# A fused decoder layer on one core: divisions of cross attention in odd steps behind two masks, roundings moved in self attention, square roots behind the second maxima

## The chip, the cores and the metric

One Trainium2 chip, one of its cores. The metric is the time of one execution in device microseconds (us); three executions of a kernel give a median. The engines are TensorE (PE), VectorE (DVE), ScalarE (ACT), GpSimd (POOL) and SyncE (SP), which here only issues transfers. Inputs lie in device memory; PE writes into PSUM, the others mostly into SBUF.

## The reference

A decoder layer on x of 4 x 512 tokens x 512, float32:

```python
x = layernorm(x + attn(x, wq, wk, wv, wo))            # 16 heads of 32, rotary, causal, 8 k/v heads
x = layernorm(x + xattn(x, ctx_512, Wq, Wkv_expand, Wout))   # 16 heads, context of 1601 x 128,
                                                             # only its first 512 keys pass the causal mask
w1, w2, w3 = (nf4_roundtrip(w) for w in (weight1, weight2, weight3))   # 1408 x 512 each
x = layernorm(x + (silu(x @ w1.T) * (x @ w2.T)) @ w3.T)
```

The selection of key blocks in self attention keeps all of them, so both attentions are softmax(q k / sqrt(32) + causal mask) v. `nf4_roundtrip` quantises the three weights: 64 values share a scale, scales are quantised to int8, and each value goes to the nearest of 16 levels, which takes 15 comparisons.

## The kernel before

The work is cut in 8 blocks b of 512 tokens: 0 to 3 are the self attention of the four sequences, 4 to 7 their cross attention (`crossed(b)` is b >= 4, `late(b)` is b >= 3). A block has 8 steps p, one for each pair of heads; a step is written (b, p) here. The feed-forward part, 4 tiles of tokens by 11 of hidden units, follows (7,7). Beside the attention of a step run pieces of other blocks' work: projections of the next block, the output projection and layer norm of the block before, and the quantisation of the weights. Every engine has its own program, written out by hand in a fixed order and tied to the others by semaphores, so an instruction that waits holds up all that stands behind it on its engine.

A step on PE, in order: the transposed scores of its units 0 and 1 (`scores`, L1014, a unit is one head's half of the queries, with the row's maximum subtracted by an extra row of the stack), maxima 0 of the step two further on (`maxima`, L978: scores whose row maximum DVE takes), the last two units of the step before weighted with the values (`weigh`, L1041), the maxima turned into rows (L1002), maxima 1, scores 2 and 3, then the projection of the next block in two halves (`make`, L962 to L964) with maxima 2 and 3 ahead of, between or behind the halves, weigh 0 and 1, and last the rounding (`rounding`, L1159: 16 small matmuls in bf16 that add up the comparisons' results). The banks of `att_scores_T` are two; scores, turned maxima, projections and roundings go through them as a ring (`ring_order`), and each must be emptied by ACT or DVE first.

DVE takes the maxima (L1653 in self attention, L1648 with the mask in cross attention), the reciprocals of the sums (`sums_of`, `over_sums`, L1660 to L1671), its share of the comparisons (`exceeds`, L1808), the layer norm: the square root by some 14 steps on 128 x 4 numbers (`begin_spread`, `end_spread`, L2054 to L2079) and the scaling (`scale_rows`, L1704). ACT has the exponentials (`exponential`, L1461, four in a step), the copies of sums (L1469) and of projections (L1386, L1399), and the other comparisons (`exceed`, L1439). The comparisons need rows that SP loads (`load_rows4`, L512) ahead of each rounding. POOL has the causal masks of cross attention (`keep_causal`, L842, one for each exponential), the division by the sums (`weighed`, L806, L808, L810), the rotary products, the division of the weights by their scales, and, in block 7, casts for the feed-forward part (L858).

SP issues the transfers of the stacks, six for each pair (`load_stacks`, L491 to L499, upper parts first, then lower), the rows, the results of the rounding (L525) and others, in the order of its program. `round_steps` (L104) gives the roundings to steps: 20 in self attention, the others in cross attention.

## Time and profile before

| | us |
|---|---|
| median of three executions | 1119.15 |
| lowest, highest | 1118.89, 1129.97 |
| the profiled execution: its own time | 1125.64 |
| its span in the trace | 1123.9 |
| PE busy | 1038.3 |
| DVE, ACT, POOL busy | 755.5, 482.4, 439.8 |

The profile is of one execution. An engine's idle time ahead of an instruction is given with what released it. TensorE's clock is granted by the chip at one of two levels, 1.2 or 2.4 GHz; the profile shows it as a share of the full one, 0.50 or 1.00, and over the whole execution it is 0.976. Matmuls are pipelined, so the spans of two that follow each other overlap.

### The profile page before, as it was taken

To read this page: it belongs to the slowest core of one execution; us is meant where nothing else is said; L and a number is where in the kernel's file an instruction comes from. 1 tells how busy PE (TensorE), PEld (TensorE's weight loads), DVE (VectorE), ACT (ScalarE), POOL (GpSimd) and SP (SyncE) were. 2 spreads that over 40 slices of the span, in tenths; PEclk is the share of its full clock that TensorE was granted. 3 is DMA by queue.
4 is the path that set the end of the run, shared out by engine and by line. 5 is a ranking of instruction groups with operands and counts; after the bars stand their busy time and mean duration, and the time that the engine had idled before them with its cause. 6 is when DMAs were issued, how large, how long until landed. Compare 5 with 4: busy or idle time off the path is not lost.

```text
span 1123.9 us, 17522 instructions
## 1 busy us (share of the span) xinstructions
PE 1038.3 (92%) x6280; PEld 670.4 (60%) x6280; DVE 755.5 (67%) x1560; ACT 482.4 (43%) x587; POOL 439.8 (39%) x462
## 2 busy tenths in 40 slices
PE   9899999999999898998989998998989999999995
PEld 7545455555455454565546556555636888888884
DVE  7778658666866688559676876877673546464535
ACT  3343445554464464546654664676442212112110
POOL 3448675975786564123352432334257000000000
PEclk9899999999999999999989999999989999999998
DMA  6731586386636674646755485757445202011021
GB/s 232 216 91 30 140 220 180 90 242 179 191 84 169 189 203 102 160 92 147 208 140 125 116 202 127 166 147 183 111 135 163 83 1 105 8 38 38 1 75 38
DMA packets 92618, 145.16 MB, mean 129 GB/s; under 512 B 22507, under 2 KB 39795, under 8 KB 92275
## 3 DMA queue, kind: packets, MB, share of 16 engines
q1 hardware_dynamic: 83218, 116.49, 39.8%
q0 software_dynamic: 8000, 26.75, 8.3%
q8 instruction: 51, 0.84, 0.3%
q10 hardware_dynamic: 1312, 0.79, 0.2%
q14 instruction: 37, 0.30, 0.1%
HBM read 78.09 MB, written 23.73 MB: 91 GB/s over the span
## 4 chain that ended last, share of the span: by engine, by line
PE 67%; DVE 19%; issue 5%; DMA 3%; POOL 3%; ACT 2%; SPq 1%; ACTq 0%; DVEq 0%; POOLq 0%
PE att_pv L1041 11%; PE att_scores L978 7%; PE att_scores L1294 7%; PE att_pv L1294 7%; PE att_scores_T L1324 7%; PE att_scores_T L962 6%; PE att_scores_T L1014 5%; PE att_scores_T L964 5%; PE att_scores_T L963 5%; DVE att_mx L1653 4%; PE att_scores_T L1159 2%; DVE att_scores L1648 2%; DVE att_nf_zone L1808 2%; DMA att_nf_home<-nf_reciprocals 2%; DVE att_stats L1684 1%
## 5 line engine op out<-in xcount | busy, mean ns | idle before, releaser
L1461 ACT ACTIVATE att_probs<-att_scores_T 128x1024 f32<-128x1024 f32 (+2 forms) x256 | 218.3, 885 | 161.7 <-PE att_scores_T L1014 159.1
L1041 PE MATMUL att_pv<-att_probs,att_v 128*32 128x512 f32 (+3 forms) x1024 | 216.6, 539 | 7.9 <-POOL att_probs L842 7.1
L1041 PE MATMUL att_pv<-att_probs,att_ones 128*32 128x512 f32 (+3 forms) x1024 | 216.6, 539 | 0.0
L1653 DVE TENSOR_REDUCE att_mx<-att_scores 128x2 f32<-128x1024 f32 x124 | 151.5, 1222 | 86.1 <-PE att_scores L978 85.3
L978 PE MATMUL att_scores<-att_k_stack,att_q_stack 96*128 96x256 f32 (+1 forms) x504 | 168.8, 407 | 32.2 <-DVE att_mx L1653 23.1
L1648 DVE CUSTOM_DVE_ANT_0 att_scores<-att_scores,att_cmask 128x128 f32<-128x128 f32 (+3 forms) x256 | 120.9, 511 | 40.6 <-PE att_scores L978 39.4
L1014 PE MATMUL att_scores_T<-att_q_stack,att_k_stack 97*128 97x512 f32 (+2 forms) x512 | 140.3, 386 | 7.7 <-ACT att_raw L1399 2.3
L978 PEld LDWEIGHTS att_scores<-att_k_stack,att_q_stack 96*128 96x128 f32 x504 | 88.3, 195 | 80.5 <-DVE att_mx L1653 32.8
L842 POOL TENSOR_SCALAR_AFFINE_SELECT att_probs<-att_probs 128x256 f32<-128x256 f32 x128 | 59.0, 461 | 164.8 <-ACT att_probs L1461 159.5
L1014 PEld LDWEIGHTS att_scores_T<-att_q_stack,att_k_stack 97*128 97x128 f32 x512 | 87.7, 195 | 49.4 <-issue 18.9
L1547 ACT ACTIVATE att_probs<-att_scores 128x512 f32<-128x512 f32 x44 | 26.3, 598 | 208.0 <-PE att_scores L1294 208.0
L1041 PEld LDWEIGHTS att_pv<-att_probs,att_v 128*32 128x32 f32 x1024 | 48.4, 112 | 107.3 <-issue 80.0
L1971 DVE TENSOR_TENSOR att_probs<-att_probs,att_pv 128x512 f32<-128x512 f32 x44 | 30.2, 687 | 110.0 <-PE att_pv L1294 110.0
L806 POOL TENSOR_TENSOR att_pv_raw<-att_pv_raw,att_sums_turned 128x512 f32<-128x512 f32 x32 | 42.1, 1315 | 90.7 <-DVE att_sums_turned L1671 72.1
L1439 ACT ACTIVATE att_nf_zone<-att_probs,att_nf_limits 128x1408 bf16<-128x1408 bf16 x37 | 54.2, 1464 | 39.2 <-DMA att_probs<-nf_x 39.2
L962 PE MATMUL att_scores_T<-att_x_hi,att_w_hi 128*128 128x512 f32 x144 | 58.7, 408 | 0.2 <-ACT att_probs L1461 0.2
L962 PE MATMUL att_scores_T<-att_w_hi,att_o_hi 128*128 128x512 f32 x128 | 52.1, 407 | 7.0 <-ACT att_probs L1461 3.8
L964 PE MATMUL att_scores_T<-att_x_hi,att_w_lo 128*128 128x512 f32 x144 | 56.8, 394 | 0.0
L963 PE MATMUL att_scores_T<-att_x_lo,att_w_hi 128*128 128x512 f32 x144 | 56.7, 394 | 0.0
L964 PE MATMUL att_scores_T<-att_w_hi,att_o_lo 128*128 128x512 f32 x128 | 50.7, 396 | 0.0
L963 PE MATMUL att_scores_T<-att_w_lo,att_o_hi 128*128 128x512 f32 x128 | 50.6, 395 | 0.0
L1399 ACT ACTIVATE att_raw<-att_scores_T 128x1024 f32<-128x1024 f32 x35 | 35.8, 1024 | 32.7 <-PE att_scores_T L964 32.7
(262 smaller groups left out, 2102.3 us busy)
## 6 DMA issues: line engine op xcount, KB each, us to landing
att_q_stack<-att_q_hi SPq DMA_DIRECT2D x128, 128.0 KB, 3.2
att_probs<-nf_x SPq DMA_DIRECT2D x28, 352.0 KB, 3.5
att_nf_home<-nf_reciprocals POOLq DMA_DIRECT2D x48, 176.0 KB, 4.8
att_q_stack<-att_q_lo SPq DMA_DIRECT2D x64, 128.0 KB, 3.6
att_k_stack<-att_k_hi SPq DMA_DIRECT2D x64, 128.0 KB, 3.5
att_nf_home<-nf_x SPq DMA_DIRECT2D x20, 352.0 KB, 3.6
w_nf<-att_nf_zone SPq DMA_DIRECT2D x192, 22.0 KB, 2.5
att_k_stack<-att_k_hi SPq DMA_DIRECT2D x64, 64.0 KB, 4.1
```

Source lines behind the costliest of these rows:

```text
L842: pool.affine_select(out=v, in_=v, compare_op=ALU.is_ge, fill=0.0, base=0, pattern=[[0, 2], [1, P]], channel_multiplier=-1).then_inc(kept, 1)
L962: T.matmul(out, a_hi, b_hi, start=start, stop=False)
L963: T.matmul(out, a_hi, b_lo, start=False, stop=False)
L964: return T.matmul(out, a_lo, b_hi, start=False, stop=stop)
L978: last = T.matmul(sco[:, r, 0:width], qst[0:96, s, r, P * t:P * t + P], kst[0:96, r if crossed(b) else 0, s, 0:width], start=True, stop=True)
L1014: last = T.matmul(bank[:, at:at + S - q0], kst[0:97, r if crossed(b) else 0, s, P * t:P * t + P], qst[0:97, s, r, q0:S], start=True, stop= ...
L1041: last = T.matmul(pv[HD * j:HD * j + HD, sums, q0:S], lhs, pr[:, at:at + S - q0], start=(t == 0), stop=(t == TT - 1))
L1294: last = T.matmul(bank, ffn_weight(w, f, kt), x[:, kt, :], start=kt == 0 and i == 0, stop=kt == KT - 1 and i == 1)
L1324: last = T.matmul(fpy[:, t, :], h[:, g % 2, P * t:P * t + P], ffn_rows(f), start=f == 0 and i == 0, stop=f == FT - 1 and i == 1)
L1461: A.activation(probs_of(b, r)[:, 1024 * h:1024 * h + w], bank[:, 0:w], ACT.Exp, scale=SCALE).then_inc(st_free, 1)
L1648: V.tensor_tensor_reduce(out=sco[:, r, 0:width], in0=sco[:, r, 0:width], in1=cmask[:, S - width:S], scale=1.0, scalar=NEG, op0=ALU.add, op ...
L1653: V.tensor_reduce(mx[:, p % 2, :].rearrange("p (r t) -> p r t", r=2)[:, :, t], sco[:, :, :], AX.X, ALU.max).then_inc(sc_free, 1)
```

## The change

1. `round_steps`: in blocks 1 to 3 pair 0 is left out, in place of pair 5. The roundings of (2,0) and (3,0) go; (1,5) and (2,5) get one, and those between move up by one.
2. SP, (4,5), (5,5), (6,5): the four transfers of the upper parts of the next block's first stack are issued ahead of the rows, the two of the lower parts stay behind.
3. POOL, cross attention: the division goes from the end of an even step (2, 4, 6) to the odd step behind it, between masks 0, 1 and masks 2, 3.
4. PE, start: 15 matmuls of the identity with itself, whose result nothing reads, in groups of five ahead of maxima 1, 2 and 3 of (0,1).
5. PE and DVE, block 3: maxima 2 stand ahead of the projection and maxima 3 between its halves, as in cross attention; on DVE they are taken before sums and comparisons.
6. ACT, cross attention, pairs 3 and 6: the first comparison goes behind exponential 3.
7. DVE: in blocks 1 and 2 the square root stands whole behind maxima 0 and 1 of pair 2, and the scaling at the step's end; in block 3 at pair 3, behind maxima 1 and 2, with the scaling of (3,4) in halves behind maxima 2 and behind the comparisons.

```diff
@@ round_steps
-            if b < B and p == 5 or b == B - 1 and p > 4 or (b, p) in ((1, 0), (B, 0)):
+            if b < B and p == 0 or b == B - 1 and p > 4 or (b, p) == (B, 0):
@@ SP
-            def load_stacks(b, p):
+            def load_stacks(b, p, parts=(0, 1)):
...
-                for lo in range(2):
+                for lo in parts:
...
+                    if fresh and crossed(b):
+                        load_stacks(*nxt, (0,))
...
                     if fresh:
-                        load_stacks(*nxt)
+                        load_stacks(*nxt, (1,) if crossed(b) else (0, 1))
@@ POOL
                         keep_causal(b, p, 0)
                         keep_causal(b, p, 1)
+                        if p > 1 and p % 2:
+                            weighed(pairs(b, p) // 2 - 1)
...
                         keep_causal(b, p, 2)
                         keep_causal(b, p, 3)
-                    if p % 2 == 0 and pairs(b, p) > 2 or (b, p) == (0, 3):
+                    if p % 2 == 0 and pairs(b, p) > 2 and not (crossed(b) and p > 0) or (b, p) == (0, 3):
                         weighed(pairs(b, p) // 2 - 1)
@@ PE
             for t in range(1, TT):
+                for i in range(5):
+                    T.matmul(bank_for(("exp", 0, 0, 0))[:, 0:P], ident[:, :], ident[:, :], start=True, stop=True)
                 maxima(0, 1, t)
...
-                    elif crossed(b) and whats:
+                    elif late(b) and whats:
@@ ACT
-                    elif 0 in mine:
+                    behind = crossed(b) and p in (3, 6)
+                    if mid is None and 0 in mine and not behind:
                         exceed(end, 0)
                     exponential(b, p, 3)
+                    if mid is None and 0 in mine and behind:
+                        exceed(end, 0)
@@ DVE
                         moments(b - 1, 1)
-                        if not late(b):
-                            begin_spread(range(TT))
...
-                    if b > 0 and not late(b) and p == 2:
-                        end_spread(range(TT))
-                    if b == B - 1 and p == 3:
-                        begin_spread(range(TT))
-                    if (b, p) == (B - 1, 4) or (b, p) == (NB - 1, 5):
+                    if (b, p) == (NB - 1, 5):
                         scale_rows(range(0, 2), TT - 1)
                     if fore:
                         maxima(*fore, 1)
...
                     if b > 0 and not late(b) and p == 2:
-                        scale_rows(range(TT), TT - 1)
-                    quick = crossed(b) and bool(made(b + 1, p))
+                        spread(range(TT))
+                    quick = late(b) and bool(made(b + 1, p))
                     if quick:
                         maxima(*fore, 2)
-                    if crossed(b) and p == 3:
-                        begin_spread(range(TT))
                     if late(b) and p == 3:
-                        end_spread(range(TT))
+                        spread(range(TT))
...
-                    if quick and b > B and p == 5:
+                    if quick and (b > B and p == 5 or (b, p) == (B - 1, 4)):
                         scale_rows(range(0, 2), TT - 1)
...
                     exceeds(end, (1, 2, 3) if beside else (3,))
...
+                    if b > 0 and not late(b) and p == 2:
+                        scale_rows(range(TT), TT - 1)
```

How the rows stand, at three places. First DVE in step (1,2); (2,2) is alike. `att_newton` is the square root, `att_mx` the maxima. Before:

```order
L2075 SCALAR_TENSOR_TENSOR att_newton<-att_newton 128x4 [waits att_seq]
L2077 TENSOR_TENSOR att_newton<-att_newton 128x4 [waits att_seq]
L2079 SCALAR_TENSOR_TENSOR att_newton<-att_newton 128x4 [waits att_seq]
L1653 TENSOR_REDUCE att_mx<-att_scores 128x2 [waits att_sc_full]
L2075 SCALAR_TENSOR_TENSOR att_newton<-att_newton 128x4 [waits att_seq]
L2077 TENSOR_TENSOR att_newton<-att_newton 128x4 [waits att_seq]
L2079 SCALAR_TENSOR_TENSOR att_newton<-att_newton 128x4 [waits att_seq]
L2075 SCALAR_TENSOR_TENSOR att_newton<-att_newton 128x4 [waits att_seq]
L2077 TENSOR_TENSOR att_newton<-att_newton 128x4 [waits att_seq]
L2079 SCALAR_TENSOR_TENSOR att_newton<-att_newton 128x4 [waits att_seq]
L1653 TENSOR_REDUCE att_mx<-att_scores 128x2 [waits att_sc_full,att_seq]
L1704 TENSOR_SCALAR att_y<-att_y,att_mean_var,att_newton 128x512 x4
```

Now, with line numbers of the changed kernel:

```order
L1696 BN_STATS att_stats<-att_y 128x6
L1665 TENSOR_REDUCE att_mx<-att_scores 128x2 [waits att_sc_full] x2
L2058 MEMSET att_newton 128x4 [waits att_seq]
L2060 BN_AGGR att_mean_var<-att_stats 128x2 x4
L2067 TENSOR_SCALAR att_newton<-att_mean_var 128x4 [waits att_seq]
L2069 TENSOR_SCALAR att_newton_int<-att_newton 128x4 [waits att_seq]
L2071 TENSOR_SCALAR att_newton<-att_newton_int 128x4 [waits att_seq]
L2079 SCALAR_TENSOR_TENSOR att_newton<-att_newton 128x4 [waits att_seq]
L2081 TENSOR_TENSOR att_newton<-att_newton 128x4 [waits att_seq]
L2083 SCALAR_TENSOR_TENSOR att_newton<-att_newton 128x4 [waits att_seq]
L2079 SCALAR_TENSOR_TENSOR att_newton<-att_newton 128x4 [waits att_seq]
L2081 TENSOR_TENSOR att_newton<-att_newton 128x4 [waits att_seq]
```

The maxima that stood between the steps of the root and behind them stand ahead of it, and the scaling of `att_y` has gone from here to behind the last comparison of the step.

Second SP in step (4,5). `att_probs<-nf_x` are the rows, `w_nf<-att_nf_zone` the results of the rounding before. Before:

```order
L512 DMA att_probs<-nf_x 128x1x1408 [waits att_piece_out1,att_piece_out0,att_st_full]
L525 DMA w_nf<-att_nf_zone 32x352 [waits att_round_ok]
L525 DMA w_nf<-att_nf_zone 32x352 x3
L519 DMA att_probs<-nf_dequantised_rows 128x352 [waits att_dqr_out1]
L491 DMA att_q_stack<-att_q_hi 32x2x512 [waits att_st_free,att_st_full]
L491 DMA att_q_stack<-att_q_hi 32x2x512
L495 DMA att_k_stack<-att_k_hi 32x2x512 x2
L491 DMA att_q_stack<-att_q_lo 32x2x512 [waits att_cross_raw_cut]
L495 DMA att_k_stack<-att_k_lo 32x2x512
L669 DMA att_y<-w_cross 128x4x512 [waits att_y_out]
```

Now:

```order
L491 DMA att_q_stack<-att_q_hi 32x2x512 [waits att_st_free,att_st_full]
L491 DMA att_q_stack<-att_q_hi 32x2x512
L495 DMA att_k_stack<-att_k_hi 32x2x512 x2
L512 DMA att_probs<-nf_x 128x1x1408 [waits att_piece_out1,att_piece_out0,att_st_full]
L525 DMA w_nf<-att_nf_zone 32x352 [waits att_round_ok]
L525 DMA w_nf<-att_nf_zone 32x352 x3
L519 DMA att_probs<-nf_dequantised_rows 128x352 [waits att_dqr_out1]
L491 DMA att_q_stack<-att_q_lo 32x2x512 [waits att_cross_raw_cut,att_st_full]
L495 DMA att_k_stack<-att_k_lo 32x2x512
```

The first four transfers of the stack stand ahead of the rows; the last two stay.

Third POOL from (7,2) to (7,5), with the casts L858 (L860 now) between. AFFINE_SELECT is the masks, four to a step. Before:

```order
L842 AFFINE_SELECT att_probs<-att_probs 128x2x128 [waits att_probs_kept,att_st_free] x4
L806 TENSOR_TENSOR att_pv_raw<-att_pv_raw,att_sums_turned 128x512 [waits att_o_ok,att_o_over_sums]
L808 CAST att_o_hi<-att_pv_raw 128x512 [waits att_o_divided]
L810 TENSOR_TENSOR att_o_lo<-att_pv_raw,att_o_hi 128x512 [waits att_o_hi_ok]
L858 CAST att_w_hi<-att_rope_tab 128x1024 [waits att_ffn_w_ok,att_ffn_w_in1]
L842 AFFINE_SELECT att_probs<-att_probs 128x2x128 [waits att_probs_kept,att_st_free] x4
L858 CAST att_w_lo<-att_rope_tab 128x1024 [waits att_ffn_w_ok,att_ffn_w_in2]
L858 CAST att_w_lo<-att_c_in 128x1024 [waits att_ffn_w_ok,att_ffn_w_in0]
L842 AFFINE_SELECT att_probs<-att_probs 128x2x128 [waits att_probs_kept,att_st_free] x4
```

Now:

```order
L844 AFFINE_SELECT att_probs<-att_probs 128x2x128 [waits att_probs_kept,att_st_free] x4
L860 CAST att_w_hi<-att_rope_tab 128x1024 [waits att_ffn_w_ok,att_ffn_w_in1]
L844 AFFINE_SELECT att_probs<-att_probs 128x2x128 [waits att_probs_kept,att_st_free] x2
L808 TENSOR_TENSOR att_pv_raw<-att_pv_raw,att_sums_turned 128x512 [waits att_o_ok,att_o_over_sums]
L810 CAST att_o_hi<-att_pv_raw 128x512 [waits att_o_divided]
L812 TENSOR_TENSOR att_o_lo<-att_pv_raw,att_o_hi 128x512 [waits att_o_hi_ok]
L844 AFFINE_SELECT att_probs<-att_probs 128x2x128 [waits att_probs_kept,att_st_free] x2
L860 CAST att_w_lo<-att_rope_tab 128x1024 [waits att_ffn_w_ok,att_ffn_w_in2]
L860 CAST att_w_lo<-att_c_in 128x1024 [waits att_ffn_w_ok,att_ffn_w_in0]
L844 AFFINE_SELECT att_probs<-att_probs 128x2x128 [waits att_probs_kept,att_st_free] x6
```

Before, the division (the three rows on `att_pv_raw`, `att_o_hi`, `att_o_lo`) stands between the masks of two steps; now it stands between the first and the second two of the odd step.

## Rows read from the trace of the kernel before

**Rows 1.** The page's first part: busy us (share of the span) and instructions.

```profile
PE 1038.3 (92%) x6280; PEld 670.4 (60%) x6280; DVE 755.5 (67%) x1560; ACT 482.4 (43%) x587; POOL 439.8 (39%) x462
```

**Rows 2.** Waits of PE: us in total, times, longest us.

```profile
PE att_scores L978 <- DVE att_mx L1653: 23.1, 33, 1.9
PE att_scores_T L1159 <- DVE att_probs L1808: 9.3, 16, 1.0
PE att_pv L1041 <- POOL att_probs L842: 7.1, 6, 2.0
PE att_scores L978 <- DMA att_k_stack<-att_k_lo: 2.5, 2, 1.4
```

**Rows 3.** Windows: length, busy us of PE, PEld, DVE, ACT, POOL; granted clock; DMA.

```profile
38.20:48.40 10.20, 8.32 (x21) 5.00 (x25) 7.34 (x11) 4.91 (x7) 0.00 (x0) 0.50 0.92 324
290.80:294.20 3.40, 3.40 (x12) 1.49 (x10) 3.33 (x8) 2.82 (x3) 1.52 (x1) 0.50 0.59 153
816.50:819.90 3.40, 2.96 (x16) 0.59 (x16) 3.06 (x11) 0.00 (x0) 2.19 (x4) 0.50 0.99 175
```

**Rows 4.** Timeline, PE at the start: start us, us, engine, line, operation.

```profile
1.59 6.65 PE L1185 MATMUL att_scores<-att_ident 128*128 128x128 f32 x32 [1.59 <-POOL att_ident L726]
...
36.92 0.73 PE L978 MATMUL att_scores<-att_k_stack,att_q_stack 96*128 96x512 f32 x2 [1.32 <-DVE att_mx L1653]
```

**Rows 5.** Timeline, block 2, pair 2.

```profile
288.95 0.15 DVE L2075 SCALAR_TENSOR_TENSOR att_newton<-att_newton 128x4 f32<-128x4 f32 x1
289.09 0.73 PE L978 MATMUL att_scores<-att_k_stack,att_q_stack 96*128 96x512 f32 x2 [1.34 <-DVE att_mx L1653]
```

**Rows 6.** Timeline, PE in steps (2,0) and (3,1).

```profile
260.42 0.33 PE L1159 MATMUL att_scores_T<-att_nf_zone,att_nf_steps 128*32 128x352 bf16 x4 [1.42 <-DVE att_nf_home L1808]
...
388.65 0.51 PE L962 MATMUL att_scores_T<-att_w_hi,att_o_hi 128*128 128x512 f32 x1 [1.79 <-POOL att_o_lo L810]
```

**Rows 7.** Timeline, PE in steps (3,3) and (3,4).

```profile
427.26 0.73 PE L978 MATMUL att_scores<-att_k_stack,att_q_stack 96*128 96x512 f32 x2 [1.21 <-DVE att_mx L1653]
...
439.95 0.74 PE L978 MATMUL att_scores<-att_k_stack,att_q_stack 96*128 96x512 f32 x2 [1.67 <-DVE att_mx L1653]
```

**Rows 8.** Timeline, steps (4,5) and (4,6).

```profile
540.42 1.00 ACT L1399 ACTIVATE att_raw<-att_scores_T 128x1024 f32<-128x1024 f32 x1
541.52 0.57 SPq L512 DMA_DIRECT2D att_probs<-nf_x  x1
...
545.56 1.46 ACT L1439 ACTIVATE att_nf_zone<-att_probs,att_nf_limits 128x1408 bf16<-128x1408 bf16 x1
...
553.02 0.50 PE L978 MATMUL att_scores<-att_k_stack,att_q_stack 96*128 96x256 f32 x2 [1.13 <-DMA att_k_stack<-att_k_lo]
```

**Rows 9.** Timeline, block 7, pairs 3, 5 and 7.

```profile
816.94 1.07 PE L1041 MATMUL att_pv<-att_probs,att_v 128*32 128x512 f32 x2 [1.88 <-POOL att_probs L842]
...
820.26 1.02 PE L978 MATMUL att_scores<-att_k_stack,att_q_stack 96*128 96x512 f32 x2 [0.18 <-DVE att_mx L1648]
...
833.80 1.07 PE L1041 MATMUL att_pv<-att_probs,att_v 128*32 128x512 f32 x2 [0.76 <-POOL att_probs L842]
...
843.04 1.29 POOL L806 TENSOR_TENSOR att_pv_raw<-att_pv_raw,att_sums_turned 128x512 f32<-128x512 f32 x1 [0.65 <-DVE att_sums_turned L1671]
843.74 2.92 ACT L1461 ACTIVATE att_probs<-att_scores_T 128x896 f32<-128x896 f32 x4 [1.88 <-PE att_scores_T L1014]
...
846.31 2.02 POOL L842 TENSOR_SCALAR_AFFINE_SELECT att_probs<-att_probs 128x256 f32<-128x256 f32 x4
...
847.31 1.07 PE L1041 MATMUL att_pv<-att_probs,att_v 128*32 128x512 f32 x2 [1.29 <-POOL att_probs L842]
```

**Rows 10.** Timeline, DVE's comparisons beside POOL and alone.

```profile
570.55 2.29 DVE L1808 TENSOR_SCALAR att_nf_zone<-att_probs,att_nf_limits 128x1408 bf16<-128x1408 bf16 x2
570.55 1.27 POOL L810 TENSOR_TENSOR att_o_lo<-att_pv_raw,att_o_hi 128x512 fp32r<-128x512 f32 x1
...
584.23 1.08 DVE L1808 TENSOR_SCALAR att_nf_zone<-att_probs,att_nf_limits 128x1408 bf16<-128x1408 bf16 x2
```

4 lines of the change are left out of this document (1 added, 3 removed).

## The prediction

> **What bounds the kernel now.** I read the page's busy times first: TensorE (PE) is busy 1038.3 us of 1123.9, so what a change can win is idle time of PE, its half-speed time, or nothing [rows 1]. PE's waits come next. The largest is for the second maxima, L1653 on VectorE (DVE), 23.1 us in 33 pieces; then 9.3 us for the comparisons of the rounding (L1808), 7.1 us in six pieces for the causal masks on GpSimd (POOL, L842), and 2.5 us in two pieces for the stacks [rows 2]. Each is an upper bound of what its part of the change can win. Third come the windows: in short stretches PE's clock is granted at 0.50, the lower of its two levels, 1.2 in place of 2.4 GHz [rows 3]. Each stood behind a gap: 1.32 us twice before 38.2, 1.34 us before 290.8, 1.88 us at 816.5 [rows 4, 5, 9]. A short stretch is 3.4 us long with PE busy all of it, so it costs 3.4 / 2 = 1.7 us where PE bounds. Nine more such stretches lie at 58.7, 389.8, 441, 553.7, 574.1, 656.1, 833.6, 847.2 and behind the end. So each gap that goes is priced twice: itself, and 1.7 us if a stretch stood behind it. Not every such gap had one: 1.42, 1.79 and 1.21 us are read below, and only the second was followed by one.
>
> The profiled execution took 1125.64 us, 6.5 above the median of 1119.15. I sum against the profile and subtract 6.5 at the end. Steps are written (block, pair).
>
> **A. Fifteen filler matmuls at the start.** The warming matmuls are the same operation: 16 of them in 6.65 us, at 0.50, so 0.42 each, 0.21 at full clock [rows 4]. Three groups of 5 are 1.04 us each. The first group stands where PE did not wait, so it delays everything by about 1.0. The other two fall into the two gaps of 1.32 [rows 4]. What they buy is the clock: the stretch from 38.2 is 10.2 us long with 8.3 us of matmuls [rows 3], 4.2 us at full clock. PE then waits for DVE and ScalarE (ACT) more often. DVE's 7.3 us of work in it sets how short it can get, 10.2 - 7.3 = 2.9 saved; none if it stays low, though then the fillers, twice as long, cost 2.1 for the first group. Bounds -1.9 and +2.1; I take **-1.5**, since three groups fill most of both gaps.
>
> By the Trainium skill ("TensorE: Matmul & The Clock Gate", Why this matters for your kernels) the clock drops only for PE-idle gaps above about 3 us; by it the fillers buy nothing and this part costs their 1.0. The trace disagrees: the longest of PE's waits is 2.0 us [rows 2], and the clock fell behind gaps of 1.3 to 1.9 [rows 3 to 5, 9].
>
> **B. Rounding moved off pair 5 in blocks 1 and 2, on to pair 0 skipped.** Twenty roundings stay. (2,0) and (3,0) lose a rounding of 0.8 us of matmuls and the wait ahead of it, 1.42 at 260.4 [rows 6] and a like one in (3,0); (1,5) and (2,5) get one each, with its row load, its comparisons and its stores on SyncE (SP). Removed 2 x 2.2 = 4.4, added 2 x (0.8 + a wait between 0 and 1.5). But in (3,1) PE waits 1.79 us for POOL's L810 [rows 6], and POOL there waits for its own transfers, so what (3,0) gains is lost again. Bounds -2.8 and +1.5; I take **-0.5**.
>
> **C. Square root behind the second maxima, blocks 1 and 2.** At 288.95 DVE runs the small steps of the root ahead of the maxima; PE then waits 1.34, and the low stretch at 290.8 follows [rows 5, 3]. In the new order three maxima stand ahead of the root and the scaling behind the comparisons. Removed in (2,2): 1.3 + 1.7 = 3.0; in (1,2) some 0.6 without a stretch. The same DVE work now stands ahead of maxima 3 and the sums, and bounds the loss at 1.0 for two steps. Bounds -3.6 and +1.0; I take **-2.6**.
>
> **D. Block 3 in the order of cross attention.** The gaps of 1.21 in (3,3) and 1.67 in (3,4) go [rows 7], the second with a stretch at 441. In their place the rounding waits: DVE does maxima 2, sums, comparisons, maxima 3 and one more comparison before it, two maxima later than now, at 1.2 us each. (3,2) has no gap today and gets one of about 1.5; in (3,4) about 2.2 comes back. Bounds: -1.2 - 1.7 - 1.7 = -4.6 if nothing comes back, +3 if both waits come and the stretch stays. I take **+0.5**.
>
> **E. Upper parts of the next stack ahead of the rows, (b,5) of blocks 4 to 6.** Rows' load L512 goes out at 541.52, at once when the rounding before it is done; the stack's first source is free when ACT has copied it, 540.42 + 1.00 = 541.42, no earlier. So four issues of 0.62 us now stand ahead, and the rows leave 2.5 us later. ACT uses them at 545.56, only just landed (3.96 us from issue) [rows 8]. Behind that comparison on ACT stand the fourth exponential, a second comparison and the two copies of the projection; those free the bank in which PE forms the next scores. So PE gets it 2.2 us later. On the other side the last lower part leaves at the same time as now, since as many issues stand ahead of it, but behind fewer bytes, and the stack's gap, 1.13 at 553.02 and 1.4 in block 5 [rows 8, 2], is covered by the new wait. So +2.2 - 1.13 = +1.1, +0.8, and in block 6, which has no stack gap, +2.2: together +4.1; a stretch stays behind each of the first two. If rows land as early as now: -1.13 - 1.4 - 2 x 1.7 = -5.9. If a new stretch comes in block 6 too: +5.8. I take **+3.5**.
>
> **F. Division in odd cross steps, behind two masks.** A division is three POOL instructions, from 843.04 until the masks start at 846.31 [rows 9], 3.3 us. Now masks 0 and 1 wait for it, afterwards masks 2 and 3. Block 7: (7,5) loses its 0.76 gap and the stretch, -2.4, for the second pair of masks is wanted late there. In (7,3) the 1.88 gap goes [rows 9], but the root's small steps on DVE now run beside the division all the way, and today already PE waits 0.18 at 820.26 for the maxima behind them. So the gap moves there: -0.5. In (7,7) nothing is left of the step to hide masks 2 and 3: of the four exponentials of 0.73 from 843.74 two belong to masks 0 and 1, so these end at 845.9, the division at 849.2 and mask 2 at 849.7; PE, with four pairs of matmuls of 0.43 at full clock from 846.0, is ready at 847.7. A new wait of 2.0 stands for the 1.29 that goes, started 1.29 earlier: -0.5. (4,7): 1.98 of gap shrinks, -0.8. Blocks 5 and 6: 0.6 each goes, 0.8 comes: +0.3. Comparisons and root beside the division in (b,3) and (b,7): +1.2. The price is read at 570.55: two comparisons take 2.29 beside POOL's L810, 1.08 alone [rows 10]. Sum **-2.7**. If every mask wait goes with its stretches: -7.1 - 4 x 1.7 = -13.9. If none and each of seven overlaps costs 1.2: +8.4.
>
> The Trainium skill ("SBUF — State Buffer", Who interferes with whom) says that a DVE instruction in a two-port mode and a GpSimd one block each other whole. The pair of rows at 570.55 agrees; by its text small single-input steps would not be held, while the rows of the root beside the division are.
>
> **G. One comparison behind the fourth exponential in pairs 3 and 6**: 1.46 us of ACT, released exponential earlier, masks earlier; bounds -1.5 and +0.5, taken **-0.2**.
>
> Sum: -1.5 - 0.5 - 2.6 + 0.5 + 3.5 - 2.7 - 0.2 = -3.5. 1125.6 - 3.5 = 1122.1 in the profile's terms, 1115.6 as a median.
>
> **Rivals.**
> 1. *The rows decide* (slower). All three steps (b,5) lose the full 2.5 us, and the wait of PE passes 1.3 us, so a stretch of 1.7 stands behind each: 3 x 4.2 = 12.6 in place of 3.5. It decides from the moment the rows land after ACT's third exponential (545.6 now, so with any delay over 0.2 us). For: no slack in that row; against: DVE comparisons may run first, and PE has projection work to do. Sum +5.6: 1124.8. With D's and F's upper bounds as well it would pass 1130.
> 2. *All stretches at changed places vanish* (faster). A -1.9, C -3.6, E -5.9, F -9 (block 7's three gaps and stretches), the rest as above: about -20, 1099. For: each stretch stands behind a gap that the change addresses; against: (7,3) and (7,7), where the gap only moves.
> 3. *The clock does not hang on these gaps.* The stretches stay where they are, fillers cost 1.0, gaps alone count: A +1.0, C -1.2, E +3.5, F -1.3, others 0: +2.0, 1121.2. Against: every stretch stands behind a gap; for: gaps of 1.42 and 1.21 had none. The page on the clock gate named above stands nearest to this one.
> 4. *Nothing moves*: PE runs on as now, as each gap turns into the next wait: 1119.
>
> **How the numbers follow.** Forecast 0.45, the rows 0.2, all vanish 0.13, no link to gaps 0.12, nothing 0.1. A measurement tells about 1%, 11.2 us: below 1108 or above 1130. Faster gets the second rival and a tail of the forecast, 0.18; slower the tail of the first and of F's contention, 0.1. The range leaves out the far part of either: 1104 to 1127.
>
> **What would show it.** After: no low stretch near 290; the fillers' two gaps filled and the clock at 1.00 through 38 to 48 (A); PE's masks row (L842) down from 7.1 to under 4, and the one left in (7,7) behind masks 2 and 3 (F); ACT idle before its first comparison at (4,5), (5,5), (6,5) for some 2 us with the rows as releaser, and no wait of PE for the k stack (E); the rounding's wait row up from 9.3 (D). Wrong if the stretches come elsewhere in the same number, or if ACT shows no such wait.

## The result and the profile after

The changed kernel takes 1154.11 us (median of four runs, 1148.11 to 1157.44); the kernel before took 1120.52 beside it. The ratio is 1.0255, 95% interval 1.0214 to 1.0296: slower by 2.6%. I had forecast 1115.6 and no change.

Below, a gap is idle time of PE ahead of an instruction, and a stretch is a time in which its clock was granted at 0.50. PE's busy time and waits in the changed kernel (us in total, times, longest), which answer to [rows 1] and [rows 2]; L1820 is the old L1808, L1665 the old L1653, L844 the old L842:

```profile
PE 1055.0 (91%) x6310; PEld 682.6 (59%) x6310; DVE 755.0 (65%) x1560; ACT 482.0 (42%) x587; POOL 430.5 (37%) x462
```

```profile
PE att_scores_T L1164 <- DVE att_probs L1820: 16.4, 14, 2.8
PE att_scores_T L1164 <- DVE att_nf_home L1820: 16.0, 6, 4.3
PE att_scores L983 <- DVE att_mx L1665: 15.5, 28, 1.9
...
PE att_pv L1046 <- POOL att_probs L844: 3.0, 2, 2.4
```

The two targets shrank as meant: maxima from 23.1 to 15.5, masks from 7.1 to 3.0. But the rounding's waits for DVE's comparisons grew from 12.2 (9.3 and 2.9) to 32.4. All gaps of PE over 0.15 us add up to 87.1 us, 71.9 before. Busy PE grew by 17 us although its work grew by 3, the fillers; the other 14 are matmuls that ran slower. Outside the end the trace has 88.7 us at 0.50, 47.8 before. So of the 31.8 us by which the profiled execution is longer, some 15 are waits, 3 fillers and 14 low clock. That is about a third of a us for each us at 0.50, not the half at which I priced it: over the 17 traces of this case PE's busy time without the fillers rises by 0.35 to 0.38 us for each us at 0.50 (a fitted line, an estimate, since the ends of matmuls are modelled). The trace is of the slowest of the four executions (1157.44 us, mean granted clock 0.958; the others have 0.961 to 0.971), so it holds more low clock than the median one.

Laid step beside step, most of the loss comes in three places: (1,5) and (2,5) grew from 8.8 to 14.9 and 14.5 us, (1,3) and (2,3) by 1.5 and 4.2, and (3,2) to (3,6) by 10.7 together. The timeline of (1,5):

```profile
224.46 2.37 POOL L781 TENSOR_TENSOR att_k_lo<-att_turned,att_k_hi 128x1024 fp32r<-128x1024 f32 x1
225.53 4.29 DVE L1820 TENSOR_SCALAR att_nf_zone<-att_nf_home,att_nf_limits 128x1408 bf16<-128x1408 bf16 x2
...
226.96 2.47 POOL L791 TENSOR_TENSOR att_turned<-att_raw,att_rope_tab 128x1024 f32<-128x1024 f32 x1
...
230.87 1.52 DVE L1820 TENSOR_SCALAR att_nf_home<-att_nf_home,att_nf_limits 128x1408 bf16<-128x1408 bf16 x1
232.09 2.52 POOL L796 TENSOR_TENSOR att_turned<-att_turned,att_swapped 128x1024 f32<-128x1024 f32 x1
232.54 1.07 PE L1164 MATMUL att_scores_T<-att_nf_zone,att_nf_steps 128*32 128x352 bf16 x12 [4.29 <-DVE att_nf_home L1820]
```

Two comparisons that take 1.08 us alone [rows 10] take 4.29 (singly 1.69 and 2.68), and each ends 0.4 us after a product of POOL: the first waits out L781 (to 226.83), the second L791 (to 229.43). PE idles as long, 4.29 us, and its clock is low afterwards. The windows behind the waits of the rounding in (1,5), (2,5), (3,3) and (3,4), 4.29, 3.87, 3.17 and 2.50 us, to be read as [rows 3]:

```profile
232.10:238.90 6.80, 6.36 (x32) 3.25 (x36) 3.25 (x4) 1.94 (x2) 6.50 (x7) 0.50 1.02 289
354.90:361.70 6.80, 6.31 (x32) 3.26 (x36) 3.25 (x4) 1.94 (x2) 6.42 (x7) 0.50 0.64 182
450.50:457.30 6.80, 5.71 (x30) 2.71 (x34) 4.86 (x7) 1.94 (x2) 0.00 (x0) 0.50 0.38 106
467.60:474.40 6.80, 6.43 (x34) 2.91 (x38) 5.40 (x7) 1.94 (x2) 4.76 (x5) 0.50 0.24 55
```

In (2,3) the scaling of the layer norm, which takes 1.91 us in (1,3) and 3.24 here, stands ahead of the rounding's last instruction on DVE (L1834), which frees the bank for PE's scores:

```profile
307.74 3.24 DVE L1716 TENSOR_SCALAR att_y<-att_y,att_mean_var,att_newton 128x512 f32<-128x512 f32 x4
...
312.63 0.50 DVE L1834 SCALAR_TENSOR_TENSOR att_nf_zone<-att_scores_T,att_nf_home 128x352 bf16<-128x352 f32 x1
...
313.19 0.73 PE L1019 MATMUL att_scores_T<-att_q_stack,att_k_stack 97*128 97x512 f32 x2 [2.51 <-DVE att_nf_zone L1834]
```

And in (3,3) the whole root, maxima 2 and 3 and three comparisons precede the rounding, slowed beside POOL: L2067 takes 1.36 us beside POOL's L816, 0.17 in the median of its 13.

```profile
441.83 2.55 POOL L816 TENSOR_TENSOR att_w_lo<-att_rope_tab,att_w_hi 128x512 fp32r<-128x512 f32 x2
...
443.06 1.36 DVE L2067 TENSOR_SCALAR att_newton<-att_mean_var 128x4 f32<-128x4 f32 x1
...
447.41 1.53 POOL L764 TENSOR_TENSOR att_nf_home<-att_nf_home 128x704 bf16<-128x704 bf16 x1 [1.55 <-DMA att_nf_home<-nf_reciprocals]
447.48 2.34 DVE L1820 TENSOR_SCALAR att_nf_zone<-att_nf_home,att_nf_limits 128x1408 bf16<-128x1408 bf16 x2
...
449.74 1.21 DVE L1665 TENSOR_REDUCE att_mx<-att_scores 128x2 f32<-128x1024 f32 x1
450.88 0.57 DVE L1820 TENSOR_SCALAR att_nf_home<-att_nf_home,att_nf_limits 128x1408 bf16<-128x1408 bf16 x1
451.59 1.07 PE L1164 MATMUL att_scores_T<-att_nf_zone,att_nf_steps 128*32 128x352 bf16 x12 [3.17 <-DVE att_nf_home L1820]
```

### The profile page after: what moved, and what is told of

Same layout as the page of the kernel before. It is cut to its first block, busy times and chain, and to the rows that moved or that the text cites. A ratio compares the mean times of both kernels' runs of the same rounds, so it can differ in the third digit from the quotient of the medians.

```text
span 1155.7 us, 17583 instructions
## 1 busy us (share of the span) xinstructions
PE 1055.0 (91%) x6310; PEld 682.6 (59%) x6310; DVE 755.0 (65%) x1560; ACT 482.0 (42%) x587; POOL 430.5 (37%) x462
## 4 chain that ended last, share of the span: by engine, by line
PE 67%; DVE 16%; DMA 5%; issue 4%; POOL 3%; ACT 3%; ACTq 0%; SPq 0%; DVEq 0%; POOLq 0%
PE att_pv L1046 11%; PE att_scores L983 7%; PE att_scores L1302 7%; PE att_pv L1302 7%; PE att_scores_T L1332 7%; PE att_scores_T L1019 6%; PE att_scores_T L967 6%; PE att_scores_T L969 5%; PE att_scores_T L968 5%; DVE att_mx L1665 3%; DMA att_nf_home<-nf_reciprocals 3%; DVE att_nf_zone L1820 2%; PE att_scores_T L1164 2%; DVE att_scores L1660 2%; DMA att_probs<-nf_x 1%
## 5 line engine op out<-in xcount | busy, mean ns | idle before, releaser
L1046 PE MATMUL att_pv<-att_probs,att_v 128*32 128x512 f32 (+3 forms) x1024 | 220.5, 547 | 3.2 <-POOL att_probs L844 3.0
L1665 DVE TENSOR_REDUCE att_mx<-att_scores 128x2 f32<-128x1024 f32 x124 | 151.6, 1223 | 107.2 <-PE att_scores L983 106.5
L1046 PE MATMUL att_pv<-att_probs,att_ones 128*32 128x512 f32 (+3 forms) x1024 | 220.4, 547 | 0.0
L983 PE MATMUL att_scores<-att_k_stack,att_q_stack 96*128 96x256 f32 (+1 forms) x504 | 171.5, 416 | 24.8 <-DVE att_mx L1665 15.5
L1019 PE MATMUL att_scores_T<-att_q_stack,att_k_stack 97*128 97x512 f32 (+2 forms) x512 | 148.9, 405 | 11.6 <-DVE att_nf_zone L1834 5.1
L983 PEld LDWEIGHTS att_scores<-att_k_stack,att_q_stack 96*128 96x128 f32 x504 | 91.2, 202 | 72.2 <-DVE att_mx L1665 27.2
L844 POOL TENSOR_SCALAR_AFFINE_SELECT att_probs<-att_probs 128x256 f32<-128x256 f32 x128 | 56.6, 442 | 206.2 <-ACT att_probs L1469 203.5
L1019 PEld LDWEIGHTS att_scores_T<-att_q_stack,att_k_stack 97*128 97x128 f32 x512 | 92.8, 206 | 56.5 <-issue 18.1
L1164 PE MATMUL att_scores_T<-att_nf_zone,att_nf_steps 128*32 128x352 bf16 x576 | 32.2, 330 | 32.7 <-DVE att_probs L1820 16.4
L1164 PEld LDWEIGHTS att_scores_T<-att_nf_zone,att_nf_steps 128*32 128x32 bf16 x576 | 14.6, 98 | 63.3 <-issue 45.3
```

What stands on the lines that cost most here:

```text
L983: last = T.matmul(sco[:, r, 0:width], qst[0:96, s, r, P * t:P * t + P], kst[0:96, r if crossed(b) else 0, s, 0:width], start=True, stop=True)
L1019: last = T.matmul(bank[:, at:at + S - q0], kst[0:97, r if crossed(b) else 0, s, P * t:P * t + P], qst[0:97, s, r, q0:S], start=True, stop= ...
L1046: last = T.matmul(pv[HD * j:HD * j + HD, sums, q0:S], lhs, pr[:, at:at + S - q0], start=(t == 0), stop=(t == TT - 1))
L1164: last = T.matmul(bank[32 * j:32 * j + 32, 0:CW], nsteps[:, 32 * k:32 * k + 32], passes[k][:, CW * j:CW * j + CW], start=k == 0, stop=k == 3)
L1665: V.tensor_reduce(mx[:, p % 2, :].rearrange("p (r t) -> p r t", r=2)[:, :, t], sco[:, :, :], AX.X, ALU.max).then_inc(sc_free, 1)
```

## The experiments

Ratios are to the kernel before, run on the same chip beside the experiment, with their 95% intervals; the changed kernel's is 1.0255 (1.0214 to 1.0296). A difference of 0.1% is 1.1 us. The changed kernel was not run again beside the experiments, so they are compared with it by these ratios: the intervals of experiments 1, 2 and 9 lie clear of its own, that of experiment 8 touches it, and those of 3 to 7 and 10 overlap it, so there the traces tell more than the times.

**1. Roundings back** (s1). Edit of the changed kernel:

```diff
-            if b < B and p == 0 or b == B - 1 and p > 4 or (b, p) == (B, 0):
+            if b < B and p == 5 or b == B - 1 and p > 4 or (b, p) in ((1, 0), (B, 0)):
```

> The changed kernel with the roundings on their old steps (pair 5 of blocks 1 to 3 left out again, pair 0 of blocks 2 and 3 used). Theory 1: the moved roundings cost about 12.6 us of the 33 (steps (1,5) and (2,5) grew by 6.1 and 5.7, (1,6) and (2,6) by 1.1 each, (2,0) and (3,0) gave back 2.3 and 2.7, (2,1) took 2.8), because the comparisons of DVE stand beside POOL's rotary products there; so about 1142. Theory 2: the waits at (1,5) and (2,5) of 4.3 and 3.9 us are a delay that DVE carries from the moved root and scaling and would come out at another rounding; then the time stays above 1150.

1141.19 us, 1.0136 (1.0088 to 1.0184): 13 us come back, as theory 1 had it. (1,5) and (2,5) are 8.8 us again. The gap in (3,3), which the edit does not touch, is 4.60 in this trace where it was 3.17.

**2. Block 3 back** (s2).

```diff
-                    elif late(b) and whats:
+                    elif crossed(b) and whats:
...
-                    quick = late(b) and bool(made(b + 1, p))
+                    quick = crossed(b) and bool(made(b + 1, p))
```

and root and scaling of block 3 on DVE where they were.

> The changed kernel with block 3 in its old order (maxima 2 and 3, square root and scaling as before). Theory 1: the order of block 3 costs the 10.7 us by which its steps (3,2) to (3,6) grew, half of it waits of the rounding for DVE (3.17 and 2.50 us in (3,3) and (3,4)), half low clock behind them; so about 1143. Theory 2: the growth there comes from the roundings that arrive one step later in the pieces' pipeline (the division of the weights), and putting the order back gives less than 4 us: above 1150.

1136.72, 1.0102 (1.0062 to 1.0141): 17 us, more than the 10.7 of its steps. Part of the rest is that (3,1) lost its gap of 2.41 and the stretch too in this execution; whether the edit did that is not shown.

**3. Root back in blocks 1 and 2** (s4), with `begin_spread` and `end_spread` at their old places.

```diff
                     if b > 0 and not late(b) and p == 2:
-                        spread(range(TT))
+                        scale_rows(range(TT), TT - 1)
...
-                    if b > 0 and not late(b) and p == 2:
-                        scale_rows(range(TT), TT - 1)
```

> The changed kernel with root and scaling of blocks 1 and 2 where they were. My forecast had this edit at -2.6, so putting it back would cost 2.6: 1156.7. The trace after says otherwise: the gaps of 1.48 and 2.51 us ahead of the second scores of (1,3) and (2,3), where PE waits for the rounding's scaling on DVE behind the four L1716, are the edit's, with a low stretch behind the second: +1.5 + 4.2 - 0.6 - 2.7 = +2.4; so 1151.7, and both gaps gone while one of 1.34 comes back in (2,2).

1150.45, 1.0225 (1.0182 to 1.0268). The intervals overlap, so the 3 us are not shown by the time; the gaps are as expected: 1.48 and 2.51 gone, 1.54 back in (2,2). But the gap in (3,3), whose program is the same, grew from 3.17 to 4.48: the first small step of block 3's root (L2069 here, L2067 in the changed kernel) is now held over both instructions of POOL's L816.

```profile
433.49 2.77 DVE L2069 TENSOR_SCALAR att_newton<-att_mean_var 128x4 f32<-128x4 f32 x1
433.69 2.54 POOL L816 TENSOR_TENSOR att_w_lo<-att_rope_tab,att_w_hi 128x512 fp32r<-128x512 f32 x2
...
443.35 1.07 PE L1164 MATMUL att_scores_T<-att_nf_zone,att_nf_steps 128*32 128x352 bf16 x12 [4.48 <-DVE att_nf_home L1820]
```

With block 3 in its new order this one gap is 2.25 to 4.65 us in the traces of experiments 1, 3, 4, 5 and 10. So a part put back moves waits elsewhere by a us or more, and the costs of the parts are known no closer than that.

**4. ACT compares in pair 5** (s5).

```diff
-    return (0, 1, 3) if b < B - 1 and p in (3, 4) else (0,)
+    return (0, 1, 3) if b < B - 1 and p in (3, 4, 5) else (0,)
```

> The changed kernel, but in pair 5 of blocks 1 and 2 ACT does three of the four comparisons and DVE one, as pairs 3 and 4 have it. Theory 1 (DVE's comparisons wait there for POOL's rotary products, 4.29 us for two that take 1.08 alone): the gaps of 4.29 and 3.87 fall under 1.5 with their low stretches, 1154 - 2 x 4.5 = 1145. Theory 2 (the rounding there waits because a step without slack got one more rounding, whoever does the comparisons): ACT's two more passes of 1.46 us each end no earlier, the gaps stay above 3 us and the time at 1152 or more.

1148.63, 1.0195 (1.0148 to 1.0241): in between, and not told from the changed kernel. The gaps fell to 2.94 and 2.94, no further, because ACT's three comparisons and the last exponential follow each other without a pause, from 223.96 to 229.19. DVE was done with its one comparison at 225.33:

```profile
223.96 1.46 ACT L1447 ACTIVATE att_nf_zone<-att_nf_home,att_nf_limits 128x1408 bf16<-128x1408 bf16 x1
225.32 1.02 ACT L1469 ACTIVATE att_probs<-att_scores_T 128x1024 f32<-128x1024 f32 x1
226.22 1.47 ACT L1447 ACTIVATE att_nf_zone<-att_nf_home,att_nf_limits 128x1408 bf16<-128x1408 bf16 x1
...
227.72 1.47 ACT L1447 ACTIVATE att_nf_home<-att_nf_home,att_nf_limits 128x1408 bf16<-128x1408 bf16 x1
...
229.29 0.75 PE L1164 MATMUL att_scores_T<-att_nf_zone,att_nf_steps 128*32 128x352 bf16 x12 [2.94 <-issue]
```

So both theories hold a part: the step is short, and DVE is held up. It has no projection of the next block (pairs 2, 3, 4 and 6 have): before the change (1,5) was 8.8 us long where (1,4) was 14.6, so little time is left for the four comparisons before PE reaches the rounding.

**5. POOL nearly free in (1,5) and (2,5)** (s7). This kernel leaves out most of the rotary product of q1 and of the lower part of k0 in blocks 2 and 3.

```diff
+                w = 16 if unit[1] in (2, 3) and unit[2] == "q1" else S
...
-                pool.tensor_tensor(rsum, rsum, rsw, ALU.add).then_inc(summed, 1)
+                pool.tensor_tensor(rsum[:, :, 0:w], rsum[:, :, 0:w], rsw[:, :, 0:w], ALU.add).then_inc(summed, 1)
```

> The changed kernel, leaving out most of the rotary product of q1 and of the lower part of k0 of blocks 2 and 3 on POOL (16 columns of 512 in each half). Nothing else moves, so DVE's comparisons of (1,5) and (2,5) find POOL nearly free. Theory 1 (they wait for POOL): two of them take 1.1 to 1.4 us in place of 4.29, and the gap of 4.29 at (1,5) falls by 3 to 4 us, the one of 3.87 at (2,5) too, with low clock behind them gone: 1154 - 9 = 1145. Rival (the step is too short for a rounding whatever POOL does): the comparisons get shorter but the gap stays above 2.5 us, since ACT or the order on DVE holds it, and the time stays above 1150.

1145.39, 1.0185 (1.0121 to 1.0250): the gain of some 8 us is as theory 1 had it, but the intervals overlap. The trace tells: the first two comparisons are as short as alone, with nothing of DVE's own program changed:

```profile
223.34 1.53 POOL L764 TENSOR_TENSOR att_c_in<-att_c_in,att_nf_home 128x704 bf16<-128x704 bf16 x1
224.79 1.07 DVE L1822 TENSOR_SCALAR att_nf_zone<-att_nf_home,att_nf_limits 128x1408 bf16<-128x1408 bf16 x2
...
226.92 2.09 DVE L1822 TENSOR_SCALAR att_nf_home<-att_nf_home,att_nf_limits 128x1408 bf16<-128x1408 bf16 x1
...
229.16 0.63 PE L1166 MATMUL att_scores_T<-att_nf_zone,att_nf_steps 128*32 128x352 bf16 x12 [1.64 <-DVE att_nf_home L1822]
```

4.29 us have become 1.07 and PE's wait 1.64; in (2,5) it is 0.20. What is left in (1,5) stands behind the third comparison, 2.09 us beside POOL's L764. So POOL is the shown cause of the long comparisons, and with POOL nearly free the short step holds the rounding almost without a wait. Most of what (2,5) gained went into another wait, 3.05 us for the stack in (2,6), which was not there in the changed kernel.

**6. The last comparison ahead of maxima 3 in block 3** (s8). Point 5 of the change is right for maxima 2; in the changed kernel maxima 3 stand on DVE ahead of the last comparison alone, not of the first two.

```diff
-                    if quick:
+                    if quick and b >= B:
                         maxima(*fore, 3)
                     exceeds(end, (1, 2, 3) if beside else (3,))
+                    if quick and b < B:
+                        maxima(*fore, 3)
```

> The changed kernel, but in block 3 DVE takes maxima 3 behind its last comparison, not ahead. Putting the whole block back gave 17. Theory 1: the waits of the rounding (1.86, 3.17 and 2.50 us in (3,2), (3,3), (3,4)) are the length of DVE's queue ahead of the last comparison; with 1.2 us less in it each falls by about 1.2, and low clock with the one or the other: 3.6 to 7 us in all, 1147 to 1150. Rival: the last comparison waits for ACT's, not for DVE, and then it changes nothing but makes PE wait for maxima 3: 1154 or more.

1149.73, 1.0252 (1.0187 to 1.0318): the median lies in theory 1's range, but the time does not tell. The waits do: 1.86, 3.17 and 2.50 became 0.92, 2.75 and 1.58, and one of 1.54 came up in (3,5).

**7. Root and scaling of block 3 back, the maxima not** (d1).

```diff
+                    if b == B - 1 and p == 3:
+                        begin_spread(range(TT))
...
+                    if b == B - 1 and p == 3:
+                        end_spread(range(TT))
...
-                    if late(b) and p == 3:
+                    if crossed(b) and p == 3:
                         spread(range(TT))
```

> The changed kernel with root and scaling of block 3 where they were (begin ahead of maxima 1, end behind; scaling around maxima 1 of (3,4)), but maxima 2 and 3 in their new place. Theory 1: the maxima ahead of the comparisons are most of it (1.86 at (3,2), where no root runs), so waits of (3,3) and (3,4) fall by 1 each at most: 1150. Rival: the whole root (2.9 us slowed beside POOL) is what the rounding of (3,3) waits for: the gap of 3.17 falls under 1.5, and 8 us or more come back, 1146 or less.

1143.49, 1.0197 (1.0153 to 1.0241): 6.5 us by the ratio, 10.6 by the medians. (3,3)'s wait at the rounding of 3.17 went and one of 1.64 for the maxima stands in its place; (3,4)'s 2.50 fell to 1.58 with no stretch. That is between the two expectations, and the intervals overlap. So the root's place has some part of block 3's 17 us, a third to two thirds by these figures, and how the rest falls to the maxima is not shown.

**8. Four waits of self attention's roundings filled with matmuls** (g1).

```diff
                 passes = over + [x4]
+                for i in range({(1, 5): 16, (2, 5): 14, (3, 3): 12, (3, 4): 9}.get(ROUND_STEPS[u], 0)):
+                    T.matmul(bank[:, 0:P], ident[:, :], ident[:, :], start=True, stop=True)
                 pe.wait_ge(over_act, ACT_PASSES[u + 1])
```

> The changed kernel with matmuls of the identity, whose result nothing reads, ahead of four roundings: 16 at (1,5), 14 at (2,5), 12 at (3,3), 9 at (3,4), some 3.3, 2.9, 2.5 and 1.9 us at full clock, inside waits of 4.29, 3.87, 3.17 and 2.50. Theory 1: about half of the loss is low clock behind such waits (88.7 us of low clock outside the end in the trace after, 47.8 before: 41 / 2 = 20 us). With the waits filled the stretches of 6.8 us at 232, 355, 450 and 468 go, 27.2 / 2 = 13.6 us less: 1154 to 1140. Rival: the clock does not hang on PE being idle there, the stretches stay, and the fillers run at half speed and delay the roundings: 1154 to 1158.

1145.00, 1.0190 (1.0160 to 1.0220): 7 us by the ratio and 9 by the medians, though DVE's comparisons did not get shorter; in (1,5) they even took 5.06. Still the clock stayed full there and at the other three places:

```profile
232.10:238.90 6.80, 5.11 (x42) 2.40 (x43) 4.04 (x4) 1.94 (x2) 6.42 (x8) 1.00 0.99 277
349.00:356.00 7.00, 5.96 (x55) 4.19 (x57) 5.00 (x6) 1.94 (x2) 6.70 (x7) 1.00 0.51 122
449.00:456.00 7.00, 6.20 (x45) 2.91 (x45) 5.17 (x8) 3.42 (x5) 0.00 (x0) 1.00 0.33 103
458.00:466.00 8.00, 6.70 (x53) 3.97 (x52) 7.90 (x15) 3.43 (x5) 0.51 (x1) 1.00 0.01 2
```

The rival is out. The 13.6 expected took each us at 0.50 for half a us; at a third the four stretches of 27.2 us are worth 9, about what came. Other stretches came and went: a new one of 6.8 at 415.9, behind a new gap of 2.77 in (3,1), and one in (1,3). All in all the trace has 51.2 us at 0.50 outside the end, 37.5 fewer than the changed kernel's, and PE's busy time without the added matmuls is 12 to 13 us less.

**9. Both large parts back** (s9), the diffs of experiments 1 and 2 together.

> The changed kernel with both the roundings on their old steps and block 3 in its old order. Put back alone they gave 12.9 and 17.4 us. Theory 1, two separate causes at separate places: the gains add, 1154 - 30 = 1124, no more than 4 us above before. Rival, one of them is only large because the other one shifts the pieces and roundings that block 3 then waits for: together they give little more than the larger, 1132 to 1137.

1130.43, 1.0065 (1.0036 to 1.0094). 21 us by the ratio, within the rival's 17 to 22, and 24 by the medians: less than the 30 of the sum, though by hardly more than the noise of three differences. Against block 3 alone the gain is not told. In its trace a gap of 3.88 in (3,2) and one of 2.62 in (1,0) appear that neither kernel alone had; ahead of the first DVE's comparisons wait 2.59 us for the transfer of their rows, which a part of the shortfall may be. Some 7 us above the kernel before stay, with the other five parts of the change still in.

**10. The stack back** (s3).

```diff
-                    if fresh and crossed(b):
-                        load_stacks(*nxt, (0,))
...
-                        load_stacks(*nxt, (1,) if crossed(b) else (0, 1))
+                        load_stacks(*nxt)
```

> The changed kernel with the next stack's upper parts behind the rows again in (4,5), (5,5), (6,5). Theory 1, the step E of the prediction: the four issues make the rows land some 2.5 us late, ACT's comparison waits, and the rounding of these steps with it (the gaps of 2.82, 2.21 and 2.29 us in the trace after); steps (b,5) and (b,6) grew by 0.8, 1.3 and 3.4 us, so putting it back gives 5.5 us: 1148.6, those gaps under 0.6 and the stack's gaps of 1.1 and 1.4 back. Rival: the gaps at the rounding there come from one more comparison that DVE does late; then they stay.

1155.65, 1.0264 (1.0185 to 1.0344): nothing came back that the time could show, but the interval is 9 us to either side. The late rows were there in the changed kernel as forecast. They leave SP at 574.60 and ACT has 2.55 idle until they land. PE meets that at the rounding, behind DVE's comparison, and not at the bank of the next scores, where I had put it:

```profile
572.00 1.19 SPq L491 DMA_DIRECT2D att_q_stack<-att_q_hi  x2
573.24 1.25 SPq L495 DMA_DIRECT2D att_k_stack<-att_k_hi  x2
574.60 1.59 SPq L512 DMA_DIRECT2D att_probs<-nf_x  x1
...
579.13 1.47 ACT L1447 ACTIVATE att_nf_zone<-att_probs,att_nf_limits 128x1408 bf16<-128x1408 bf16 x1 [2.55 <-DMA att_probs<-nf_x]
...
583.20 0.70 PE L1164 MATMUL att_scores_T<-att_nf_zone,att_nf_steps 128*32 128x352 bf16 x12 [2.82 <-DVE att_probs L1820]
```

With the stack back that 2.82 is gone in (4,5), and (5,5) and (6,5) fall from 2.2 to 1.2; but (5,7) and (6,7) then wait 2.60 and 2.62 where they waited 1.29 and 1.28, (4,7) has a new gap of 1.56, and the stack's gaps of 1.1 and 1.4 did not return. Away from the edit the trace has larger gaps too: 5.04 in (1,5), 2.78 in (3,1), 4.65 in (3,3). So what the part costs stays open; the forecast's 3.5 lies within the noise.

**11 to 13. Parts alone on the kernel before,** with the lines of the change's own diff: the division's under POOL (f1), the fillers' under PE (a1), both with ACT's late comparison (c1).

> The kernel before with the division in cross attention's odd steps alone. The forecast for this part was -2.7. With fillers and the late comparison beside it, it came out 3 to 6 us slower than before. If the division is the cause (the root of block 7 beside it: a gap of 3.83 us in (7,3) with a low stretch in (7,4), and the roundings' waits of 2.59 in (6,7) and 1.2 in (b,5)), this kernel has those gaps and takes 1122 to 1126. If the fillers are, it takes 1117 to 1120.

1125.08, 1.0000 (0.9970 to 1.0030).

> The kernel before with the fifteen filler matmuls alone. The forecast for this part was -1.5, with the clock at full through 38 to 48. What the trace after showed: the two gaps of 1.32 filled, a low stretch all the same but 6.8 us long in place of 10.2, and 1.3 us lost by (0,1). So +1.3: 1122; if the fillers hold the clock in most executions it is 1118 to 1120.

1124.68, 1.0010 (0.9983 to 1.0038).

> The kernel before with only three parts of the change: the division in cross attention's odd steps, the fillers, and the comparison behind the fourth exponential. By the steps of the trace after, the division gave about 2.3 us back in all, the fillers cost about 1 and the comparison nothing: 1 to 2 us less than before, so 'same'. Theory of the prediction: -1.5 - 2.7 - 0.2 = -4.4. If either is over 1% from before, a part that I cost at nothing matters.

1127.75, 1.0034 (1.0002 to 1.0066). f1 and a1 are not told from the kernel before, and f1 came out where its first case had it. c1 is some 4 us slower, its interval just clear of 1; I had expected 1 to 2 less, and the prediction 4.4 less. In the changed kernel's trace the fillers do hold the clock full where it fell before, but it falls 6 us later behind a gap of 1.21:

```profile
38.20:44.20 6.00, 4.09 (x21) 2.78 (x20) 3.73 (x5) 2.59 (x4) 0.00 (x0) 1.00 1.05 325
44.30:51.10 6.80, 6.80 (x24) 2.74 (x24) 5.91 (x8) 2.88 (x3) 2.02 (x2) 0.50 0.49 198
```

and the division's gap in (7,3) moved, as forecast, behind the root, only twice as long as the one it replaced:

```profile
849.26 1.28 POOL L812 TENSOR_TENSOR att_o_lo<-att_pv_raw,att_o_hi 128x512 fp32r<-128x512 f32 x1
849.44 1.12 DVE L2081 TENSOR_TENSOR att_newton<-att_newton 128x4 f32<-128x4 f32 x1
...
853.74 1.31 PE L983 MATMUL att_scores<-att_k_stack,att_q_stack 96*128 96x512 f32 x2 [3.82 <-DVE att_mx L1660]
...
882.26 0.41 PE L1046 MATMUL att_pv<-att_probs,att_v 128*32 128x256 f32 x2 [2.44 <-POOL att_probs L844]
```

**14. The division in pairs 5 and 7 only** (c3), on the kernel before.

```diff
+                        if p > 3 and p % 2:
+                            weighed(pairs(b, p) // 2 - 1)
...
-                    if p % 2 == 0 and pairs(b, p) > 2 or (b, p) == (0, 3):
+                    if p % 2 == 0 and pairs(b, p) > 2 and not (crossed(b) and p > 2) or (b, p) == (0, 3):
```

> The kernel before with the division moved in pairs 5 and 7 of cross attention alone; pair 3, where DVE takes the root, keeps it at the end of pair 2. The division in all three took the time of before. In its trace (7,5) gave 3.0, (4,7) and (5,0) 3.4, and (4,3), (7,3), (7,4) took 2.4. Theory: those 2.4 stay away: 2 to 4 us less than before, 1119 to 1121. Rival: what (7,5) and (4,7) gave is lost behind (6,6) and the waits of the roundings, and it is equal to before within 1 us.

1122.32, 0.9983 (0.9958 to 1.0008): at most a little faster, not shown. It has the lowest ratio of the versions run, and none is shown to be faster than the kernel before.

**15. Root behind the second maxima, scaling behind the rounding's last instruction** (c2), on the kernel before.

```diff
                     if end is not None:
                         scale_rounded(end)
+                    if b > 0 and not late(b) and p == 2:
+                        scale_rows(range(TT), TT - 1)
```

> The kernel before with root behind the second maxima in blocks 1 and 2 alone, and with the scaling one place later than in the change, behind the rounding's last instruction on DVE (L1834 in the changed kernel). Theory: what the edit lost were the gaps ahead of the second scores of (1,3) and (2,3), where PE waits for that instruction behind four scalings; they go, and the 1.34 of (2,2) with its low stretch goes too, so 3 to 5 us less than before: 1116 to 1118. Rival: the root ahead of sums and comparisons makes the rounding of (1,2) and (2,2) wait instead, and it comes out at 1120 to 1123.

1130.40, 1.0057 (1.0031 to 1.0082): slower than before, against both theories. The scalings are taken off the bank's way and put in the maxima's. They take 4.18 us beside POOL (1.91 alone), and PE waits 3.17 for the maxima behind them:

```profile
186.50 4.18 DVE L1708 TENSOR_SCALAR att_y<-att_y,att_mean_var,att_newton 128x512 f32<-128x512 f32 x4
...
191.78 1.21 DVE L1657 TENSOR_REDUCE att_mx<-att_scores 128x2 f32<-128x1024 f32 x1
193.05 1.22 PE L978 MATMUL att_scores<-att_k_stack,att_q_stack 96*128 96x512 f32 x2 [3.17 <-DVE att_mx L1657]
```

## Why the prediction was wrong

- **B, the roundings**, -0.5 forecast, +13 measured. The step that failed is "added 2 x (0.8 + a wait between 0 and 1.5)". The waits are 4.29 and 3.87. I bounded the new wait by the waits of other pairs. Pair 5 has no projection to cover a wait, and POOL works on rotary products all the while. I named the row that shows the price (two comparisons in 2.29 beside one POOL instruction, [rows 10]) and applied it to F, where it hardly mattered, and not to B. The upper bound of +1.5 does not come out of its terms either: -4.4 + 4.6, with 2.2 lost again in (3,1), is +2.4.
- **D, block 3**, +0.5 forecast, +17 measured. "gets one of about 1.5; in (3,4) about 2.2 comes back" was right in kind (1.86 and 2.50), but (3,3) was taken as a gain of 1.2 and became a wait of 3.17, for the root, the maxima and the comparisons add up there; and I charged no low clock for the new waits. The +0.5 is not the sum of its terms either: -4.6 + 1.5 + 2.2 is -0.9, or +0.8 with the stretch kept. And "(3,2) has no gap today" was a misreading, since PE waits 1.33 us there for the second maxima:

```profile
411.28 0.73 PE L978 MATMUL att_scores<-att_k_stack,att_q_stack 96*128 96x512 f32 x2 [1.33 <-DVE att_mx L1653]
```

- **C, the root**, -2.6 forecast, +2.4 by the steps of the trace, 3 by the time of experiment 3, which is within its noise. The gap of 1.34 and its stretch went as said. Missed is what stands behind the scaling in its new place: the rounding's last instruction and with it the bank of the next scores. "bounds the loss at 1.0" had looked only at maxima 3 and the sums.
- **The clock.** The forecast priced stretches where one might go and none where a wait was added in self attention. Behind the four longest of those waits they are 6.8 us long, where I had counted with 3.4. The 41 us more at 0.50 are some 14 of the 31.8; at half a us each, as I priced them, they would be 20.
- **E, the stack**, +3.5 forecast; nothing measured, with an interval of 9. The late rows are there (2.55 on ACT, some 2 forecast; 2.82, 2.21 and 2.29 on PE, 2.2 forecast), though PE waits at the rounding and not at the bank. Part of the cost is taken back in (5,7) and (6,7), where the steps without it wait 1.3 us longer.
- **F**, -2.7 forecast, 0 measured with an interval of 3; **A**, -1.5 forecast, +1 with an interval of 3. That the gaps of (7,3) and (7,7) would only move was foreseen (the second as 2.0, it is 2.44), and (7,5) gave its 3.0; (7,3) and (7,4) lost 1.8, where I had 0.5 as a gain. **G** was never run alone.
- The rival for slower (the rows) came true in its condition: in (4,5), (5,5) and (6,5) PE waits over 2 us and a stretch follows each. But those steps and the ones behind them grew by 5.5 us in the trace and not by 12.6, and the 33 us came from elsewhere. Large new waits in self attention had no rival at all, and the range's upper end of 1127 left them out.

The Trainium skill ("SBUF — State Buffer", Who interferes with whom) says which DVE operations can share the port pair with GpSimd, `tensor_scalar` among them, and that the second to issue is blocked for the whole of the other. Experiment 5 agrees: 4.29 us with POOL busy, 1.07 with POOL free. In the prediction I read the page as sparing small single-input steps; its list has `tensor_scalar`, and L2067, 1.36 us beside POOL, is one.
